# Four more staging slots for the ternary weights, and a new order of steps, in a fused cross-attention and BitNet feed-forward kernel

## The reference

```python
x = x + tanh(g_xattn) * xattn(layernorm(x), ctx, ctx, Wq, Wk, Wv, Wo, bo, g)
x = x + tanh(g_ffn)   * ffn(layernorm(x), w_gate, w_up, w_down)

def xattn(q, k, v, ...):              # channels x positions, 8 heads of 64
    qh = softmax(Wq q over the 64 of a head) * 64 ** -0.5
    kh = softmax(Wk k over the positions)
    context = kh @ (Wv v).T           # per head, 64 x 64
    out = Wo (context.T qh) + bo
    return out / norm(out over channels) * g * sqrt(128)

def bitlinear(x, w):                  # three times: gate, up, down
    scale = mean(abs(w))              # over the whole matrix
    q = round(clip(w / (scale + 1e-5), -1, 1))
    return x @ (q * scale).T
def ffn(x): return bitlinear(bitlinear(x, w_gate) * bitlinear(x, w_up), w_down)
```

## Time and profile before

| | before |
|---|---|
| median of three runs | 1387.82 us (1387.11 to 1389.66) |
| span of the profiled execution | 1386.2 us |
| PE busy | 1314.9 us (95% of the span) |
| DVE, ACT, POOL busy | 1003.7, 634.1, 580.5 us |
| PE busy in the first 173 us | 115.2 us |
| PE busy in the other 1213 us | 1199.7 us |
| mean granted clock of PE over the span | 0.979 |
| read from and written to HBM | 152.37 MB, 25.95 MB |

### The profile page before, as it was taken

The page is one execution under the profiler, slowest core; times in us unless marked ns, Lnnn a source line. Parts: engine busy times, 40 slices in busy tenths (PEclk is TensorE's granted clock), DMA queues, the critical chain, the costliest instruction groups (busy, mean ns, idle before and its releaser), DMA issues. The chain is left out here.

```text
span 1386.2 us, 30208 instructions
## 1 busy us (share of the span) xinstructions
PE 1314.9 (95%) x12408; PEld 961.9 (69%) x12408; DVE 1003.7 (72%) x1343; ACT 634.1 (46%) x879; POOL 580.5 (42%) x357
## 2 busy tenths in 40 slices
PE   4787599999999899999999999999999999999999
PEld 2454387855787558876598757885598748985994
DVE  6977778878799976887688875889578866641330
ACT  4668786853544424453434533453344443320220
POOL 0249925866274472444334451346034432240120
PEclk8998799999999999999999999999999999999999
DMA  9939999896664879778777975787677895663421
GB/s 352 408 145 336 267 288 306 243 184 151 146 163 99 174 180 244 182 181 186 168 176 174 196 187 136 200 169 186 150 184 181 179 171 130 159 173 88 138 76 46
DMA packets 401417, 260.00 MB, mean 188 GB/s; under 512 B 325312, under 2 KB 342080, under 8 KB 401280
## 3 DMA queue, kind: packets, MB, share of 16 engines
q1 hardware_dynamic: 394368, 232.90, 67.3%
q10 hardware_dynamic: 6912, 25.17, 5.7%
HBM read 152.37 MB, written 25.95 MB: 129 GB/s over the span
## 5 line engine op out<-in xcount | busy, mean ns | idle before, releaser
L1118 PE MATMUL ps<-w_dn,inter_buf 128*128 128x512 fp8e4 x1376 | 307.8, 380 | 2.0 <-DVE inter_buf L1372 1.3
L1118 PEld LDWEIGHTS ps<-w_dn,inter_buf 128*128 128x128 f16 x1376 | 134.9, 99 | 157.8 <-issue 4.7
L1804 POOL TENSOR_TENSOR qs<-qs,q_stat 128x1024 f32<-128x1024 f32 x64 | 129.6, 2024 | 232.9 <-DVE q_stat L1615 232.9
L1034 PE MATMUL ps<-zT,w_gu 128*128 128x256 f16 x1664 | 191.2, 274 | 3.0 <-DVE zT L1372 2.4
L1034 PEld LDWEIGHTS ps<-zT,w_gu 128*128 128x128 fp8e4 x1664 | 163.0, 99 | 29.2 <-DVE zT L1372 2.6
L1069 PE MATMUL ps<-w_gu 128*128 128x128 f16 x2880 | 174.0, 219 | 2.7 <-DVE w_gu L1715 1.8
L1069 PEld LDWEIGHTS ps<-w_gu 128*128 128x128 fp8e4 x2880 | 165.8, 98 | 7.1 <-issue 3.1
L1860 POOL TENSOR_TENSOR w_gu<-w_gu 128x512 f32<-128x512 f32 x60 | 82.4, 1373 | 179.8 <-DVE w_gu L1715 112.6
L1069 PE MATMUL ps<-zT,w_gu 128*128 128x128 f16 x2176 | 132.6, 219 | 0.0
L1715 DVE SCALAR_TENSOR_TENSOR w_gu<-ps,w_gu 128x512 f32<-128x512 f32 x120 | 82.5, 688 | 68.0 <-PE ps L1069 67.9
L1069 PEld LDWEIGHTS ps<-zT,w_gu 128*128 128x128 fp8e4 x2176 | 125.5, 98 | 3.9
(11 more groups left out here) (195 smaller groups left out, 2588.8 us busy)
## 6 DMA issues: line engine op xcount, KB each, us to landing
w_gu<-forms SPq DMA_DIRECT2D x158, 256.0 KB, 3.0
ct_raw<-forms SPq DMA_DIRECT2D x52, 256.0 KB, 3.1
w_dn<-in_down_w SPq DMA_DIRECT2D x19, 512.0 KB, 6.0
xb<-in_x ACTq DMA_DIRECT2D x16, 512.0 KB, 6.8
x_dram<-xb SPq DMA_DIRECT2D x16, 512.0 KB, 3.9
fin<-x_dram SPq DMA_DIRECT2D x32, 256.0 KB, 2.9
out<-fin SPq DMA_DIRECT2D x32, 256.0 KB, 2.4
inter_buf<-in_up_w SPq DMA_DIRECT2D x15, 512.0 KB, 9.7
```

What stands on the lines that cost most here:

```text
L1034: last = nc.tensor.matmul(ps[:, rest_bank(g, j), s * T:s * T + T], w_gu[:, w, k, :], zT[:, h, k, :], start=(k == 0 and h == 0), stop=(k == ...
L1118: mm = nc.tensor.matmul(ps[:, down_bank(g, k), :], inter_of(g, j, u % 2, b), w_dn[:, j, hf * 512:hf * 512 + 512], start=(u == 0), stop=(u ...
L1804: nc.gpsimd.tensor_tensor(v, v, q_stat[:, u % 2, 1, :].unsqueeze(2).broadcast_to([P, 2 * HEADS, DH]), ALU.mult).then_inc(q_prob, 1)
```

## The change

Four more slots, 13 to 16, are laid over the last 16 KB of each partition's `w_gu` (the places of G14 to G21 and U13 to U21, which are written last). `STAY` goes from 6 to 8 chunks of gate and of up, so that 28 and not 32 of their chunks are loaded a second time. `SLOT` and `WHEN` are new as a whole: the order of steps differs on every engine, most in the first third. The mathematics, the tiles and the instructions of each step are the same, and PE has the same matmuls.

```diff
-SLOT = [0, 1, 2, 3, 4, 5, 6, 7, 8, 9, 10, 11, 12, 0, 1, 2, 3, 4, 5, 6, 7, 8, 9, 10, 11, 12, 0, 1, 2, 3, 4, 5, 6,
...
+SLOT = [14, 15, 16, 5, 6, 7, 8, 9, 10, 11, 12, 0, 1, 2, 3, 4, 13, 14, 15, 16, 5, 6, 7, 8, 9, 10, 11, 12, 0, 1,
+    2, 3, 4, 13, 14, 15, 16, 5, 6, 7, 8, 9, 10, 11, 0, 1, 2, 3, 4, 13, 14, 15, 16, 5, 6, 7, 8, 9, 10, 11, 12,
+    13, 14, 15, 16, 5, 6, 7, 8, 9, 10, 11, 12, 5, 6, 7, 8, 9, 10, 11, 12, 5, 6, 7, 8, 9, 10, 11, 12, 5, 6, 7, 8,
...
-STAY = (6, 6, 0)
+STAY = (8, 8, 0)
...
-STAGES = 13
+STAGES = 17
...
+        stage_d = w_gu[:, 2 * IC + 1 - 16:2 * IC + 1, :, :].rearrange("p w k i -> p (w k i)").bitcast(F32).rearrange(
+            "p (s c) -> p s c", s=4)
...
+            if s > 12:
+                return stage_d[rows, s - 13, cols]
```

More of the change, by code:

```diff
@@ new lines @@
+    "ld_ctx": [5, 108, 280, 451, 674, 1013, 1100, 1397, 1702, 1941, 2085, 2338, 2521, 2755, 2936],
+    "cabs": [3, 52, 162, 299, 529, 957, 1047, 1124, 1622, 1839, 2062, 2115, 2364, 2537, 2785, 2958],
+    "csum": [23, 60, 179, 327, 654, 981, 1064, 1295, 1687, 1840, 2071, 2308, 2496, 2742, 2919, 3160],
+    "cscale": [42, 66, 192, 326, 659, 984, 1051, 1302, 1673, 1852, 2079, 2326, 2503, 2748, 2923, 3164],
+    "c_hi": [208, 381, 669, 1012, 1031, 1319, 1681, 1843, 2080, 2332, 2501, 2749, 2924, 3165],
@@ new lines @@
+    "turn_k": [394, 426, 455, 530, 571, 647, 705, 738, 833, 865, 899, 924, 1041, 1083, 1163, 1229, 1231, 1312, 1340,
+        1373, 1440, 1489, 1515, 1570, 1723, 1762, 1763, 1812, 1942, 1971, 1983, 2034, 2154, 2192, 2222, 2250, 2358,
+        2377, 2416, 2468, 2579, 2614, 2643, 2672, 2779, 2799, 2839, 2890, 3001, 3036, 3065, 3095, 3195, 3213, 3261,
+        3285],
+    "ctxk": [119, 146, 232, 279, 452, 526, 687, 838, 950, 989, 1144, 1245, 1352, 1447, 1538, 1631, 1804, 1851, 1987,
+        2067, 2213, 2273, 2410, 2486, 2635, 2696, 2833, 2908, 3057, 3117, 3253, 3308],
@@ new lines @@
+    "turn_q": [474, 541, 656, 688, 748, 815, 881, 898, 916, 977, 1040, 1043, 1090, 1197, 1309, 1332, 1359, 1390,
+        1498, 1531, 1577, 1642, 1678, 1731, 1835, 1845, 1934, 1946, 1997, 2058, 2145, 2163, 2215, 2243, 2343, 2369,
+        2432, 2490, 2573, 2593, 2637, 2664, 2764, 2791, 2854, 2912, 2995, 3015, 3059, 3087, 3180, 3206, 3268, 3319,
+        3364, 3409],
+    "outp": [167, 186, 187, 188, 256, 257, 258, 259, 321, 329, 354, 362, 382, 383, 411, 412, 641, 642, 643, 644,
[6 rows of a table added]
+    "yev": [176, 273, 352, 416, 652, 724, 889, 964, 1065, 1120, 1325, 1386, 1522, 1620, 1734, 1783, 1919, 1945,
[3 rows of a table added]
@@ new lines @@
+    "ssg": [209, 283, 343, 397, 676, 772, 918, 956, 1079, 1152, 1333, 1399, 1529, 1613, 1755, 1795, 1924, 1972,
[5 rows of a table added]
+    "ld_xr": [163, 173, 613, 914, 1062, 1313, 1587, 1721, 1929, 2103, 2302, 2318, 2735, 2738, 3156, 3158],
[9 rows of a table added]
+    "zt_hi": [351, 453],
+    "zt_lo": [334, 471],
+    "z_hi": [874, 1017, 1430, 1431, 1667, 1838, 2021, 2279, 2449, 2699, 2869, 3122, 3281, 3465],
+    "z_lo": [877, 1015, 1452, 1477, 1661, 1850, 2033, 2278, 2456, 2701, 2878, 3125, 3287, 3469],
+    "turn_z": [910, 1019, 1473, 1474, 1836, 1837, 2267, 2294, 2679, 2706, 3105, 3129, 3460, 3472],
[6 rows of a table added]
@@ new lines @@
+    "store_form": [358, 359, 360, 1111, 1112, 1114, 1117, 1118, 1123, 1150, 1239, 1242, 1243, 1244, 1248, 1249,
+        1251, 1252, 1260, 1261, 1286, 1287, 1326, 1327, 1328, 1329, 1368, 1369, 1405, 1407, 1421, 1461, 1469, 1470,
+        1487],
+    "form": [344, 1115, 1153, 1154, 1155, 1160, 1161, 1172, 1264, 1265, 1294, 1305, 1306, 1341, 1342, 1379, 1384,
+        1451, 1462, 1463],
+    "load_form": [1491, 1495, 1496, 1508, 1509, 1510, 1524, 1525, 1534, 1535, 1539, 1543, 1544, 1561, 1562, 1563,
[11 rows of a table added]
@@ new lines @@
+    "l_hi": [13, 14, 15],
+    "l_lo": [81, 82, 286],
+    "wpart": [239, 240, 686],
+    "wtotal": [243, 246, 698],
+    "wscale": [241, 242, 707],
+    "consts": [8],
+    "prod": [4],
+    "gains": [10],
+    "wload": [24, 25, 26, 27, 28, 29, 30, 31, 32, 33, 34, 35, 36, 37, 38, 39, 40, 54, 55, 56, 63, 64, 67, 68, 69,
[5 rows of a table added]
+    "wsum": [21, 58, 57, 59, 65, 72, 73, 79, 80, 84, 85, 86, 87, 111, 107, 113, 112, 120, 122, 121, 131, 132, 133,
+        140, 141, 154, 155, 156, 157, 171, 169, 170, 172, 174, 180, 181, 189, 190, 210, 211, 212, 226, 213, 214,
+        504, 518, 545, 514, 547, 568, 546, 569, 573, 583, 597, 622, 629, 630, 631, 632, 645, 646, 664, 663, 666,
+        665],
```

251 lines of the change are left out of this document (101 added, 150 removed), and 194 rows, old and new, of tables (SLOT, WHEN).

## The result

| | before | changed |
|---|---|---|
| median of 20 runs | 1386.90 us (1384.01 to 1391.84) | 1394.25 us (1383.64 to 1405.71) |
| ratio to before | | 1.0049, interval 1.0031 to 1.0068 |
| span of the profiled execution | 1386.2 us | 1390.8 us |

The change makes the kernel 0.5% slower; 0.6% faster was forecast, and the median lies outside the forecast range. The second thing to see is the spread: 22 us where the kernel before has 8. The slowest of the 20 executions, 1405.71 us, counts as a slow one and is left out of the ratio; without it the spread is 19 us. The profiled execution (1392.6 us) is 1.6 us under the median.

The account below looks back on a forecast made before the run. PE was taken as the bound, with gains possible only in its opening gaps before the first gu at 173.10 us. Terms A to E summed to -8.0 us: span 1378.2, median 1380 us (-0.6%), range 1375 to 1384.

Parts of the forecast that it names:

- What bounds the kernel: Whole kernel: PE busy 1314.9 of 1386.2 us, so gains only in the opening, by an earlier first gu.
- A: Opening, DVE: up's threshold follows gate's at about 1.2 us instead of 4.22, starting POOL's list earlier; -3.0 us.
- B: POOL's list up to rstd2(1,0): three roundings fewer, one more qnorm ahead, POOL busy throughout; -1.4 us.
- rival 2: Gain spent again: POOL's late qnorm(1,0) holds batch 1's attention back, taking 4 to 7 us; 1386 us, chance 0.17.
- C: Opening, PE's wait for transposed keys: ld_ctx(4,0) no longer issued during the second transposition, which lands earlier; -3.1 us.
- D: Six matmuls of kt(3,0) move from behind the first gu into PE's wait for zT, which covers them; -1.7 us.
- E: Second loads from U10 on turn over eight slots instead of thirteen, so POOL may wait for transfers; +1.2 us.
- rival 1: Eight-slot ring stalls POOL at SP's loads U10 to U19, with transpositions in between; 1392 us, chance 0.15.
- rival 3: Larger gain: batch 0's attention moves up too, PE's 4.1 us wait for m shrinks; 1374 us, chance 0.18.

Follow-up runs that it names:

- b4_ctx4_out3: Kernel before, with the load ld_ctx(4,0) alone moved on ACT behind kf_hi(2,2), out of the transposition turn_k(2,1); 1386.37 us, ratio 1.0002 to before.
- a2_xq4: Changed kernel, with the load ld_xq(4,0) alone moved later on ACT, behind wsum(2,7); 1386.93 us, ratio 0.9994 to the kernel before.
- c1_xq4_act: a3_sp with the load ld_xq(4,0) alone put back on ACT at the changed kernel's place; 1381.28 us, ratio 0.9964 to the kernel before.
- a3_sp: Changed kernel, with loads of contexts and x from batch 4 on (ld_xr from batch 2) issued by SP, not ACT; 1379.34 us, ratio 0.9934 to before.
- c2_sp_again: a3_sp measured once more, unchanged, on another chip; 1377.17 us, ratio 0.9936 to the kernel before.
- c3_before_sp: Kernel before, with its later loads of contexts and x issued by SP in place of ACT, second measurement; 1386.06 us, ratio 0.9996 to before.
- a1_again: Changed kernel as it is, measured again for a second trace; 1392.74 us, ratio 1.0040 to the kernel before.

## Why the prediction was wrong

Taken by its own steps.

**What bounds the kernel: right in the main.** Most of PE's gaps lie in the opening, and the change did shorten them: 57.8 to 49.1 us. But "it can gain only in the opening" was wrong: the new order closed 3.7 us of gaps between 400 and 480 us.

**A, threshold of up, -3.0: the mechanism right, the size too small.** The gap between the thresholds shrank from 4.22 to 1.05 us, as forecast (1.2). But the threshold of gate came 4.1 us earlier too (89.13 for 93.19); I had let it stand, and no run shows why it moved.

**B, POOL's list, -1.4: outweighed.** From a threshold 7.2 us earlier, `z` came only 2.5 us earlier (160.48 + 1.62 = 162.10 for 164.57). POOL was taken to be busy throughout; in the changed kernel it waits in its list, in 90 to 158 us:

```profile
L1814 POOL TENSOR_TENSOR qs<-qs,q_stat 128x1024 f32<-128x1024 f32 x5 | 9.5, 1899 | 2.5 <-DVE q_stat L1625 2.5
...
L1820 POOL TENSOR_TENSOR rsv<-ssv,cst 128x4 f32<-128x4 f32 x3 | 5.0, 1679 | 4.2 <-DVE ssv L1636 4.2
```

That is rival 2 in small, 6.7 us of waits for batch 1's attention. A and B together gave 2.5 of the 4.4 forecast.

**C, the keys, -3.1: right and a little small.** `zt` starts 7.2 us earlier, 4.7 more than `z`; `turn_k(2,1)` takes 5.4 us. The load cost it more than its bytes: 4.5 us by b4_ctx4_out3, so the lower value of 1.3 us, that of the bytes, is out. The 3.1 was a middle between two readings; that it came out near 4.7 is no evidence for the middle.

**D, kt(3,0), -1.7: wrong in mechanism.** It didn't slip into the wait for `zT`; it waited there itself, 2.46 us. From the start of `zt` to the end of gu(0,0,1), with `kt(3,0)` between in both lists, PE needs 10.3 us before and 10.4 now: the move gave nothing.

**E and rival 1, the ring, +1.2: didn't happen.** POOL has no wait for a transfer between 90 and 175 us; the eight slots were enough. Of rival 3 a part came: PE's wait for `m` fell from 4.1 to 2.3 us, inside the opening's 7.1.

A to D were to give 9.2 us up to the first `gu`; gu(0,0,1) ended 7.1 us earlier (172.6 for 179.7).

These are the smaller misses, 2.1 us in all. **The step that failed** is the sentence that costs the other moved steps at nothing, "behind work of PE that is 358.97 of 367 us busy", with 1 to 2 us if that cover is gone. Among those steps are ACT's loads, which the text names only as `ld_xr`, and the one that did the first harm, `ld_xq(4,0)`, isn't named at all. The runs showed waits of PE of 5.7, 2.6 and 2.4 us in its place, and with the lower clock behind them a cost of 7.4, 4.3 and 4.2 us. That the loads on ACT are the cause is shown for the first by a2_xq4 (load moved away: 5.8 us back) and c1_xq4_act (load put back: 4.1 us lost), for all three together by a3_sp. The cover held for what the moved steps compute and not for what they do to transpositions. Term C had the evidence: one transposition at 11.2 us with a load issued 1.7 us behind it. I read it as the late neighbour of one wait, to be gained once, instead of asking of each load in the new order whether it falls into the issue of a transposition. Priced so, at 4 to 7 us of PE's time for each meeting that its lists can't absorb, the change carries a risk as large as its gain. With the meetings gone, the change gives 8.9 us (c2_sp_again beside c3_before_sp), and 8.0 were forecast; that the two are close is luck. 3.5 us of it stand at the end of gu(0,0,1), and most of the rest comes by 485 us, from stages that the sum put at nothing.

## What to carry to other kernels

Where one engine issues transposing transfers and another plain ones, look in the trace for transpositions whose landing takes over twice the median, and at what the other queue issued meanwhile; issuing both from one engine was worth 1.0% in the changed kernel and nothing measurable in the kernel before. A wide spread is worth a look, but it is a weak sign: 22 us against 8 in the first measurement were 10 against 12 in a1_again's. A wait is to be priced with what the clock does behind it: 2.4 us cost 4.2 here. And when an order is changed, each transfer that moves is to be costed against the queue beside it, even where its data are needed much later.

## What was not expected of the hardware

A load of 512 KB by ACT and a transposition by SP that meet can take 11.8 and 12.8 us where the medians of such loads and transpositions are 4.7 and 5.0, while the transfer engines show a share of 1.11 and move 117 GB/s. It doesn't happen each time: of 17 transpositions that met a load during their issue in one trace, 7 took over 9 us. In the changed kernel with SP issuing both, none took over 8.6 us; in the kernel before with the same edit one took 9.3. What in the two queues decides it, and how exact the meeting must be, stays open. Open too is whether the kernel before gains from the same edit: 1.4 and 2.7 us are left at the end of its two traces, and the ratios (0.9995 and 0.9996, from 0.9981) can neither show nor exclude that.
